# Attention with a top-6 expert layer: who makes residues, when rows are scattered, and the order of the weight splits in the merge

## The reference

```
qkv  = x @ w_qkv ; 16 heads of 16 ; q / 4
attn = softmax(q k^T, causal) v ; out = attn @ w_out
x1   = layernorm(x + out)
probs = softmax(x1 @ gate_w.T) ; idx = top_k(probs + gate_b, 6) ; cw = probs at idx
y    = sum over 16 experts of cw * ((silu(x1 W1' + b1) * (x1 W3' + b3)) W2' + b2)     (hidden 176)
z    = the same form with shared weights, hidden 352, for every token
result = layernorm(x1 + y + z)
```

## Time and profile before

| | us |
|---|---|
| median of 3 runs | 1275.85 (1274.35 to 1281.53) |
| the profiled execution's own time | 1289.9 |
| its span, first to last instruction | 1288.1 |
| busy: TensorE / DVE / ACT / POOL | 1084.9 / 729.5 / 655.4 / 801.3 |
| mean granted TensorE clock | 0.914 of full |

### The profile page before, as it was taken

The page is one execution under the profiler, slowest core; times in us unless marked ns, Lnnn a source line. Parts: engine busy times, 40 slices in busy tenths (PEclk is TensorE's granted clock), DMA queues, the critical chain, the costliest instruction groups (busy, mean ns, idle before and its releaser), DMA issues.

```text
span 1288.1 us, 29913 instructions
## 1 busy us (share of the span) xinstructions
PE 1084.9 (84%) x8039; PEld 877.5 (68%) x8040; DVE 729.5 (57%) x2365; ACT 655.4 (51%) x1656; POOL 801.3 (62%) x738
## 2 busy tenths in 40 slices
PE   4989988888787888877626999999999999999961
PEld 3536464555454554457626999999999999999861
DVE  5766847456655658547715555555554555555345
ACT  3456555646444655554403555555555555555434
POOL 3425387576858687858660456666666666666556
PEclk8789989888988988978858899999999999999985
DMA  6334254344425353366674576666666666666692
GB/s 168 109 86 105 96 147 141 98 129 126 138 95 158 126 157 116 105 215 203 227 233 154 101 115 110 118 113 115 116 113 110 113 116 117 112 116 115 124 292 98
DMA packets 125657, 172.18 MB, mean 134 GB/s; under 512 B 17664, under 2 KB 98048, under 8 KB 125568
## 3 DMA queue, kind: packets, MB, share of 16 engines
q1 hardware_dynamic: 86400, 116.67, 32.6%
q0 software_dynamic: 39168, 54.42, 21.5%
HBM read 67.43 MB, written 78.03 MB: 113 GB/s over the span
## 4 chain that ended last, share of the span: by engine, by line
PE 44%; DMA 23%; issue 11%; DVE 9%; POOL 7%; ACT 4%; SPq 1%; another core or an unknown queue 0%; POOLq 0%; ACTq 0%; DVEq 0%
DMA z_d<-y_sb,tokens 18%; PE psum L716 9%; PE psum L972 6%; PE psum L731 5%; PE psum L758 4%; PE psum L999 4%; PE psum L746 4%; DVE rowmax L1330 3%; POOL xs_d L1810 2%; PE psum L733 2%; DMA x_d<-y_sb,tokens 2%; PE psum L959 1%; PE psum L983 1%; PE psum L968 1%; ACT probs L1069 1%
## 5 line engine op out<-in xcount | busy, mean ns | idle before, releaser
L1330 DVE TENSOR_REDUCE rowmax<-psum 128x1 f32<-128x512 f32 (+3 forms) x352 | 216.3, 636 | 125.4 <-PE psum L733 116.6
L1069 ACT ACTIVATE probs<-psum 128x512 f32<-128x512 f32 (+2 forms) x384 | 182.6, 533 | 188.2 <-PE psum L746 186.5
L1892 POOL DMA_INDIRECT x_d<-y_sb,tokens x104 | 162.6, 1563 | 99.1 <-ACT y_sb L1253 86.9
L1810 POOL DMA_INDIRECT xs_d<-x1p,index x192 | 194.8, 1015 | 44.1 <-issue 41.9
L1892 POOL DMA_INDIRECT z_d<-y_sb,tokens x104 | 162.0, 1558 | 91.3 <-ACT y_sb L1253 58.1
L1645 DVE TENSOR_TENSOR xb_lo<-psum,xb_hi 128x256 fp32r<-128x256 f32 x208 | 88.3, 425 | 229.4 <-ACT xb_hi L1060 224.7
L972 PE MATMUL psum<-we_hi_lo,xb_hi 128*128 x832 | 201.9, 325 | 0.0
L731 PE MATMUL psum<-stack_k,stack_q 96*128 96x256 bf16 (+3 forms) x512 | 151.0, 332 | 54.9 <-DVE rowmax L1330 27.1
L1253 ACT ACTIVATE y_sb<-psum,combine 128x256 f32<-128x256 f32 x208 | 98.6, 474 | 183.6 <-DMA z_d<-y_sb,tokens 83.5
L999 PE MATMUL psum<-we_hi_lo,hb_hi 88*128 (+1 forms) x832 | 174.9, 302 | 0.0
L1743 POOL TENSOR_SCALAR_AFFINE_SELECT probs<-probs 128x512 f32<-128x512 f32 x128 | 82.3, 646 | 122.9 <-ACT probs L1069 121.5
(11 more groups left out here) (197 smaller groups left out, 2388.0 us busy)
## 6 DMA issues: line engine op xcount, KB each, us to landing
xb<-xs_d SPq DMA_DIRECT2D x208, 138.0 KB
w_raw<-in_we SPq DMA_DIRECT2D x16, 608.0 KB
stack_q<-q_h SPq DMA_DIRECT2D x24, 256.0 KB
stack_k<-k_h SPq DMA_DIRECT2D x24, 256.0 KB
x1T<-x1T_d SPq DMA_DIRECT2D x24, 256.0 KB
xT_raw<-in_xT SPq DMA_DIRECT2D x9, 512.0 KB, 3.7
stack_q<-q_m SPq DMA_DIRECT2D x16, 256.0 KB
stack_k<-k_m SPq DMA_DIRECT2D x16, 256.0 KB
```

Source lines behind the costliest of these rows:

```text
L1069: nc.scalar.activation(probs[kt][:, heads[0]:heads[0] + n, :], st[f % ST_BANKS][:, 0:n * width].rearrange("p (h t) -> p h t", h=n), ACT.Ex ...
L1330: nc.vector.reduce_max(rowmax[gpar][:, heads[0]:heads[0] + n, qt], src, AX.X).then_inc(sm_free, 1)
L1810: nc.gpsimd.indirect_dma_start(out=xs_d[:, :], out_offset=bass.IndirectOffsetOnAxis(ap=index[tp][:, n:n + 1], axis=0), in_=x1p[tp][:, n // ...
L1892: nc.gpsimd.indirect_dma_start(out=(x1_d, z_d)[k % 2][:, :], out_offset=bass.IndirectOffsetOnAxis(ap=tokens[:, k:k + 1], axis=0), in_=y_sb ...
```

## The change

- `rest_of` goes from GpSimd to DVE, for all four tiles; x's low half (`low_x_of`, before `split_x` on GpSimd) too. They stand behind the maxima of their sub.
- MISC: v1 before k0 and k1. Residues, middle and last parts are one or two subs later; normalize is one sub later; GpSimd's `inverse_std` moves ahead of the mask of (1, 7).
- Scatters: a table SCATTERS_AT says how many stand in a sub: 3, 4, 6 and 11 in groups 0 to 3; none in (1, 6) and (1, 7).
- No `by_two`: every engine has eight iterations written out.
- Merge: 6 weight items (3 shared, 3 experts) are split in the last batch, before it was 2; 11 stand in tiles 0 to 23, two after the last tile. The expert order is W_ORDER, the AFTER_ gates are numbers of experts; SyncE loads two items ahead. All `low` are on DVE. TABLE_TILE is 18; scatters stand in other tiles.
- `split_w`: ScalarE copies in two parts, the second scaled by row_mask (which clears the rows that hold biases in the high part); DVE's second operation on four rows is gone. The bias rows are now taken from the low part, so matmuls read another offset, and ones replace minus ones.

```diff
 MISC = {
-    (0, 0): "m", (0, 1): "q0", (0, 2): "q1", (0, 3): "v0", (0, 4): "k0", (0, 5): "k1", (0, 6): "v1", (0, 7): "t0",
+    (0, 0): "m", (0, 1): "q0", (0, 2): "q1", (0, 3): "v0", (0, 4): "v1", (0, 5): "k0", (0, 6): "k1", (0, 7): "t0",
-REST_AT = {(0, 1): 0, (0, 2): 1, (0, 4): 2, (0, 5): 3}
-PARTS_AT = {(0, 2): 0, (0, 3): 1, (0, 5): 2, (0, 6): 3}
+REST_AT = {(0, 2): 0, (0, 3): 1, (0, 6): 2, (0, 7): 3}
+PARTS_AT = {(0, 3): 0, (0, 4): 1, (0, 7): 2, (1, 0): 3}
-NORMALIZE_AT = {(2, 0): 0, (2, 1): 1}
+NORMALIZE_AT = {(2, 1): 0, (2, 2): 1}
-SPLIT_X_AT = (3, 1)
+SPLIT_X_AT, LOW_X_AT = (3, 1), (3, 3)
-SCATTER_FROM = 2
+SCATTERS_AT = {(0, 1): 1, (0, 4): 1, (0, 6): 1}
+SCATTERS_AT.update({(1, s): 1 for s in (2, 3, 4, 5)})
+SCATTERS_AT.update({(2, s): 1 for s in (0, 1, 2, 3, 6, 7)})
+SCATTERS_AT.update({(3, s): 2 if s in (2, 4, 6) else 1 for s in range(SUBS)})
-FIRST_W_AT = {(3, 4): 0, (3, 5): 1}
+FIRST_W_AT = {(0, 4): 0, (1, 0): 1, (1, 4): 2, (2, 0): 3, (2, 4): 4, (3, 0): 5}
-TABLE_TILE = 17
+TABLE_TILE = 18
-W_ITEM_AT = {0: 2, 1: 3, 2: 4, 4: 5, 5: 6, 7: 7, 8: 8, 10: 9, 11: 10, 13: 11, 15: 12, 17: 13, 18: 14, 20: 15, 23: 16,
-             25: 17}
-AFTER_SCORES, AFTER_ATTEND, AFTER_ROUTER, AFTER_RANK, AFTER_TABLES, AFTER_SCATTER = 5, 8, 12, 15, 16, 18
+W_ORDER = (0, 1, 14, 2, 3, 4, 5, 6, 7, 8, 9, 10, 11, 12, 13, 15)
+W_ITEM_AT = {0: 6, 1: 7, 3: 8, 4: 9, 6: 10, 8: 11, 10: 12, 15: 13, 18: 14, 20: 15, 23: 16}
+AFTER_SCORES, AFTER_ATTEND, AFTER_ROUTER, AFTER_RANK, AFTER_TABLES, AFTER_SCATTER = 2, 5, 9, 12, 13, 15
-LOW_ON_DVE = 17
-SCATTER_EARLY = {T: tuple(range(3 * (T - 1) // 2, 3 * T // 2)) for T in range(1, 17)}
-SCATTER_LATE = {T: (2 * (T - 17), 2 * (T - 17) + 1) for T in range(17, 29)}
+SCATTER_EARLY = {T: tuple(range(3 * (T - 1) // 2, 3 * T // 2)) for T in range(1, 9)}
+SCATTER_EARLY.update({T: (2 * T - 10, 2 * T - 9) for T in range(11, 17)})
+SCATTER_LATE = {T: tuple(range(3 * (T - 17), 3 * (T - 16))) for T in range(17, 25)}
...
+                if last:
+                    load_first_chunk()
                 load_shift(4 * b + 1, par, 1, 1)
+                if last:
+                    load_w(2)
+                    load_w(3)
...
-                    if t in W_ITEM_AT and W_ITEM_AT[t] + 1 < W_ITEMS:
-                        load_w(W_ITEM_AT[t] + 1)
+                    if t in W_ITEM_AT and W_ITEM_AT[t] + 2 < W_ITEMS:
+                        load_w(W_ITEM_AT[t] + 2)
...
-            iteration(0, 0)
-            by_two(pe, iteration, 1, LAST - 1)
-            iteration(LAST, LAST % 2)
+            for b in range(B):
+                iteration(b, b % 2)
...
-                        rows = DOWN_K if (d, a, b) == (KD - 1, 0, 0) else HK
+                        rows = DOWN_K if (d, a, b) == (KD - 1, 0, 1) else HK
...
-                    copy(w_all[:, i - ST, 0, :], w_raw[i % 2][:]).then_inc(wt_hi, 1)
+                    copy(w_all[:, e, 0, 0:W2_AT], w_raw[i % 2][:, 0:W2_AT])
+                    copy(w_all[:, e, 0, W2_AT:W_COLS], w_raw[i % 2][:, W2_AT:W_COLS], row_mask[:, 0:1]).then_inc(
+                        wt_hi, 1)
...
+            def low_x_of(nb):
+
+                dve.wait_ge(xT_hi_done, nb + 1)
+                nc.vector.tensor_tensor(XT[1][:], xT_raw[:], XT[0][:].bitcast(fp32), ALU.subtract).then_inc(
+                    xT_lo_done, 1)
...
+                        if (g, s) in REST_AT and not (whole and b == LAST):
+                            tile = REST_AT[g, s]
+                            rest_of(b + 1, tile, fill_no(b, key_of(QK[tile])))
+                        if (g, s) == LOW_X_AT and not (whole and b == LAST):
+                            low_x_of(b + 2)
```

More of the change, by code:

```diff
@@ L493, in settle @@
             eng.sem_inc(passed, 1)
-        def by_two(eng, body, first, second_last):
-            with eng.Fori(0, (second_last - first + 1) // 2) as turn:
-                for k in range(2):
-                    body(2 * turn + (first + k), (first + k) % 2)
         def moved(j0, k):
@@ L551, in iteration @@
                 sp.dma_start(x_res[:], x[b]).then_inc(xres_loaded, 16)
+                if last:
+                    load_w(4)
+                    load_w(5)
                 load_shift(4 * b + 3, par, 1, 3)
                 if last:
-                    load_first_chunk()
+                    load_w(6)
                 if not first:
@@ L967, in block_up @@
                 pe.wait_ge(x_lo_done, j0 + (k + 1))
-                nc.tensor.matmul(uv, select[0:BIAS_K, :], w_flat[0:BIAS_K, bass.ds(at + W2_AT, UP)],
+                nc.tensor.matmul(uv, select[0:BIAS_K, :], w_flat[0:BIAS_K, bass.ds(at + W_COLS + W2_AT, UP)],
                                  start=True, stop=False)
@@ L1193, in _ @@
             act.wait_ge(w_lo_done, 4)
-            iteration(0, 0)
-            by_two(act, iteration, 1, LAST - 1)
-            iteration(LAST, LAST % 2)
+            for b in range(B):
+                iteration(b, b % 2)
             def epilogue(t):
@@ L1282, in _ @@
             high(T1 - 1)
-            split_w(W_ITEMS - 1)
+            for i in range(W_IN_TILES, W_ITEMS):
+                split_w(i)
             act.wait_ge(wt_lo, W_ITEMS)
@@ L1616, in _ @@
                         split_shift(0, 0, fill_of(len(PROLOGUE)), f - 2)
-            for b in range(3):
+            for b in range(B):
                 iteration(b, b % 2)
-            by_two(dve, iteration, 3, LAST - 1)
-            iteration(LAST, LAST % 2)
             def hide(T):
@@ L1786, in iteration @@
                     for s in range(SUBS):
+                        if (g, s) == INVERSE_AT and not (whole and b == 0):
+                            inverse_std(ln_step, rstd_step, b - 1)
                         if s % 2:
@@ L1791, in iteration @@
                             misc_stage(b, g, stage, fill_no(b, (g, s)))
-                        if (g, s) in REST_AT and not (whole and b == LAST):
-                            tile = REST_AT[g, s]
-                            rest_of(b + 1, tile, fill_no(b, key_of(QK[tile])))
                         if (g, s) in PARTS_AT and not (whole and b == LAST):
                             last_part(b + 1, PARTS_AT[g, s])
-                        if (g, s) == INVERSE_AT and not (whole and b == 0):
-                            inverse_std(ln_step, rstd_step, b - 1)
-                        if (g, s) == SPLIT_X_AT and not (whole and b == LAST):
-                            split_x(b + 2)
-                        n = SUBS * g + s - SCATTER_FROM
-                        if 0 <= n < SCATTERS and not (whole and b < 2):
-                            scatter(b - 2, par, n)
+                        if (g, s) in SCATTERS_AT and not (whole and b < 2):
+                            done = sum(SCATTERS_AT[k] for k in SCATTERS_AT if k < (g, s))
+                            for n in range(done, done + SCATTERS_AT[g, s]):
+                                scatter(b - 2, par, n)
             def scatter(t, tp, n):
@@ L1849, in _ @@
             split_x(1)
-            for b in range(2):
-                iteration(b, b)
-            by_two(pool, iteration, 2, LAST - 2)
-            for b in (LAST - 1, LAST):
+            for b in range(B):
                 iteration(b, b % 2)
```

55 lines of the change are left out of this document (26 added, 29 removed).

## The result

The changed kernel takes 1237.01 us (median of 4 runs, 1231.31 to 1238.53) against 1276.14 (4 runs, 1274.35 to 1281.53): a ratio of 0.966, 95% interval 0.9624 to 0.9696, which is 39 us less. I had said 1224, range 1194 to 1254.

The account below looks back on a forecast made before the run. TensorE bounds the expert blocks (busy 501 of 514 us), booked at 0; only attention and merge can move. Attention -28 and merge -24 sum to -52 us, taking the median 1275.85 to 1224 us; 8-in-10 range 1194 to 1254.

Parts of the forecast that it names:

- Step 1: Attention group 0, batches 2 to 6: fewer residues and scatters on GpSimd end the t_lo stall, -30 us (-21 to -35).
- Step 2: Starts of batches 3, 4 and 5: written-out batches remove the loop jumps, -16 us (-7 to -19).
- Step 3: Attention: earlier inverse deviation shortens group 1 to 2, -5 us; eleven scatters in the last group booked 0, at worst +15.
- Step 4: Attention, batches 0 to 6: residues and x's low half on DVE land partly on the path, +13 us (0 to +66).
- Step 5: Attention, seven batches: later k delays the stack_k copies, so group 2 waits, +10 us (0 to +28).
- Batch 7: Last attention batch: GpSimd's scatters and masks as before, three more weight splits on DVE and ScalarE, 0 (-3 to +5).
- Step 6: Merge: cheaper splits, h_lo on DVE, shorter first x1T wait and later table tile, together -24 us.
- (b): Merge: the first x1T wait shrinks because shorter splits let DVE reach z_sb of tile 11 sooner, -3 us (0 to -7.8).
- (a): Merge: fewer, cheaper splits in tiles 0 to 17 and no TensorE wait for h_lo, -12 us (-4 to -20).
- B: Rival, 15%: in attention TensorE stands 4 us before group 2 in seven batches, waiting for the stack; 1247 us.
- A: Rival, 17%: in attention DVE's additions fall into its idle time and stack_k is in time; 1201 us.
- C: Rival, 4%: DVE becomes the bound in groups 0 and 3 of attention, the kernel gets slower; 1317 us.

Follow-up runs that it names:

- a_rest_gpsimd: The changed kernel with the four residues (rest_of) back on GpSimd in the same subs, x's low half still on DVE: 1225.32 us, 0.958 of before.
- a_even: The changed kernel with its 24 scatters spread 4, 6, 7 and 7 over the groups instead of 3, 4, 6 and 11: 1226.66 us, 0.959 of before.
- b_written_out: The kernel before with only its loops over batches written out on all five engines: 1264.98 us, 0.9926 of before.
- a_w_ahead: The changed kernel with weight loads 4 and 5 of the last batch issued ahead of x_res by SyncE: 1243.34 us, 0.9728 of before.
- a_scatters_old: The changed kernel with the scatters in their old places, one per sub from (0, 2) to (3, 1): 1227.65 us, 0.9618 of before.
- a_low_gpsimd: The changed kernel with h_lo of the first 17 merge tiles back on GpSimd, behind each tile's epilogue: 1241.23 us, 0.966 of before.
- a_loops: The changed kernel with the loops over batches of the kernel before put back: 1238.36 us, 0.9696 of before.

## Why the prediction was right, and where it was not

**Step 1** (GpSimd relieved, -30): right in mechanism and size for its own stretch. The stretches lost 104.0 - 73.7 = 30.3 us over five batches (21.2, 20.8, 20.4, 20.8 and 20.8 before, 14.75 after), and the experiments add that the scatters carry it, some three and a half to one. They also show that it is no gain of the whole: moved as the change moves them, the scatters cost the other stretches and batch 7 more than the 4 us a batch that they bring here.

**Step 2** (batches written out, -16): the jump is real, 3.8 and 4.3 us of idle time where it comes back, 7 us of stretch. (The Trainium skill, "Runtime: NRT & Kernel Launch", section "Instruction fetch mechanics", says that a taken branch to code outside the fetched window waits for a fetch; these two rows agree, though they show an idle time without a name and not a fetch.) But alone it brought 11.3 us over batches 2 to 6 (346.6 to 335.3; against the second profile 5.7), and none of it in the stretches into a new batch, where DVE's wait beside `xT_lo` had lain under the jump. The whole time fell 0.74%, 9 us. Undone in the new kernel, against `a_rest_gpsimd`, whose residues differ too, it costs 10.3 us in batches 2 to 6 (315.3 against 305.0), nearly all of it in the stretches into a new batch (91.6 against 81.0).

**Step 3** is the term that failed in attention. "I book 0" for the eleven scatters of the last group, with "up to 3 us a batch, +15" if the cover is gone: 8.4 us in batches 2 to 6 and 5.4 in batch 7 come back in `a_even`, 13.8 together. The cover was counted wrongly in one respect: I let group 0 work the lag off, but in batches 3 to 6 the stretch into the new batch lies ahead of that, and batch 7 has no next batch. The -5 for the norm did not come: group 1 to 2 is 16.5, 15.8, 14.4, 15.2 and 16.0 after and 16.3, 15.9, 14.8, 15.8 and 16.1 before, the shift rows standing where the norm's lag had been. With the old places of the scatters it is 13.1 to 13.9.

**Step 4** (DVE takes over, +13) was too dear. The grouped rows of DVE in batches 2 to 6 of the changed kernel, mean ns behind the comma:

```profile
L1379 DVE TENSOR_TENSOR rest<-rest,k_h 128x512 f32<-128x512 f32 x10 | 8.0, 797 | 7.2 <-issue 5.5 <-ACT rest L1064 1.6
...
L1379 DVE TENSOR_TENSOR rest<-rest,q_h 128x512 f32<-128x512 f32 x10 | 7.0, 701 | 0.0
L1385 DVE TENSOR_TENSOR xT_lo<-xT_raw,xT_hi 128x1024 fp32r<-128x1024 f32 x5 | 6.1, 1210 | 0.0
```

A residue is 0.70 to 0.80 us, near the lower end of the earlier trace rows and not at the 1.1 that I took, and x's low half 1.21. That is 4 x 0.75 + 1.21 = 4.2 us a batch in place of 5.8, and group 0 to 1 at 14.8 with TensorE busy 14.5 leaves it nothing on the path. Only batch 1 shows any price: 14.8 us against 13.9. The rule weighed there (the Trainium skill, "SBUF — State Buffer", section "SBUF: two separate sides") would show as stretched residues; at a mean of 0.75 they seldom met GpSimd's tensor work. Elsewhere the traces agree with it, and there it counts: `gate` at 2.85 us beside GpSimd's `xT_lo` in `b_written_out`, a meeting that the change removes, and the weight split of 4.23 us beside t_lo in `a_w_ahead`. The prediction had the rule as a loss of GpSimd's gain; what it lacked is the gain for DVE when x's low half leaves GpSimd.

**Step 5** (k later, +10): the wait came as described, 1.89 to 2.84 us in batches 1 to 6 (315.30 above is one) and 5.24 in batch 0 (4.77 in the earlier trace rows). Its cause is open: in batch 1, where the copies did come earlier, k's place did not make it, and in batches 2 to 6 they were not brought forward. The sums up to batch 2 are +0.8 in the first pair of profiles and +4.1 in the second, not +7, so in batches 0 and 1 the steps 4 and 5 cost less than booked.

**Batch 7** (0, -3 to +5): +6.9, by step 3's scatters.

**Step 6** (merge, -24): right in what moves, too large by 6 to 12. On the first chip, from `b_written_out` (before's merge) to `a_scatters_old` and `a_rest_gpsimd`, it is 132.5 to 114.3 and 114.4, so -18; on the third 136.2 to 124.0, -12; in my profile pair -13.7. In the first case the one large wait is for x1T, 14.14 and 16.17 us, at the tile I named (I had said 12 to 15). In the other two there is no x1T wait but ScalarE's stalls, which nothing in the trace of before had priced. The longer one stands over the time of that wait: the load behind the pads was issued at 631.77 us, before the stall ended at 634.70. Which term was too large is open. On the first chip the two x1T waits go from 8.61 and 13.51 us to 4.00 and 14.14 (`a_scatters_old`), so (b) came at about its size; `a_low_gpsimd` puts no clear price on h_lo's place, a part of (a), and the splits were not tested alone.

**Blocks** (0): the first pair of profiles shows 13 us less, but that is no gain of the change that could be shown. ScalarE's waits in this stage, in before, in after and in `after_again`, which is the same kernel as after (total, times, longest):

```profile
ACT y_sb L1253 <- DMA z_d<-y_sb,tokens: 83.5, 86, 2.2
ACT y_sb L1253 <- DMA x_d<-y_sb,tokens: 72.1, 74, 1.4
```

```profile
ACT y_sb L1261 <- PE psum L1003: 88.1, 155, 0.8
```

```profile
ACT y_sb L1261 <- DMA z_d<-y_sb,tokens: 86.3, 87, 2.0
ACT y_sb L1261 <- DMA x_d<-y_sb,tokens: 75.0, 78, 1.5
```

The 156 us in which ScalarE waited for scatter-adds to land are absent in after's first profile, 71 in its second, and 161 in its third. From the first block's transposition to the last, the stage takes 479.3, 482.1 and 492.6 us in these three, 490.9 and 492.7 in the two of before, 484.3 in `b_written_out` and 488.4 in `a_loops`. So equal code differs by 13 us here from one execution to another, and the difference of the first pair is no proof of a gain. What decides it, and whether the change makes the shorter form more frequent, is open.

The medians differ by 39 us and not 52. What is short is the merge (10 to 12 us) and batch 7 (7). In batches 2 to 6 the sum was met (-34.4 or -39.6 for -35) partly by luck: the cost of step 3 and the missing -5 of the norm and most of step 2 were made up by cheaper steps 4 and 5 and by DVE's stall beside `xT_lo`, which I had not seen. Of the rivals, B's wait for the stack came at half its size, and A's free DVE was nearly right; C did not begin, since the maxima release TensorE at most 1.4 us late in after.
